# Four layer norms of a graph network: the last step moved to ScalarE, with the engines' sequences laid anew

## What is computed

```python
x = _layernorm(x + _L0_gnn_ref(x, adj, ...))   # attention, 4 heads of 64, masked by adj
x = _layernorm(x + _L1_gnn_ref(x, adj, ...))   # 4 heads: tanh of masked scores, times Wh, relu, then a gate
x = _layernorm(x + _L2_gnn_ref(x, adj, ...))   # 8 heads of 32: softmax cut where the cosine is at most 0.1
x = _layernorm(x + _L3_gnn_ref(x, adj, ...))   # attention, 4 heads of 64, masked by adj

def _layernorm(x, axis=-1, eps=1e-05):
    m = jnp.mean(x, axis=axis, keepdims=True)
    v = jnp.var(x, axis=axis, keepdims=True)
    return (x - m) / jnp.sqrt(v + eps)
```

## Time and profile before

| | us |
|---|---|
| median of 3 runs | 2612.17 |
| lowest, highest | 2611.11, 2615.91 |
| the profiled execution | 2615.28 |
| its span in the trace | 2613.5 |
| busy PE, DVE, ACT, POOL in it | 2549.5, 2006.1, 1394.8, 915.9 |

### The profile page before, as it was taken

One profiled execution on the slowest core, in us unless ns is written; L12 is line 12 of the kernel. 1 busy time (PEld: TensorE's weight loads), 2 busy tenths in 40 slices (PEclk: granted clock), 3 DMA queues, 4 the chain that ended last, 5 costly groups with the idle time before them and its releaser, 6 DMA issues.

```text
span 2613.5 us, 62943 instructions
## 1 busy us (share of the span) xinstructions
PE 2549.5 (98%) x21905; PEld 2283.8 (87%) x21905; DVE 2006.1 (77%) x6661; ACT 1394.8 (53%) x3893; POOL 915.9 (35%) x987
## 2 busy tenths in 40 slices
...
DMA packets 44490, 29.90 MB, mean 11 GB/s; under 512 B 21264, under 2 KB 44048, under 8 KB 44432
## 3 DMA queue, kind: packets, MB, share of 16 engines
...
## 4 chain that ended last, share of the span: by engine, by line
PE 83%; ACT 4%; DVE 3%; issue 1%; POOL 0%; DVEq 0%; ACTq 0%; POOLq 0%
PE bank L471 21%; PE bank L473 19%; PE bank L472 19%; ACT arena L603 4%; PE bank L1439 4%; PE bank L528 4%; PE bank L537 3%; PE bank L460 3%; PE bank L1429 3%; PE bank L548 2%; PE bank L1419 2%; PE bank L1450 2%; DVE arena L687 1%; DVE b L644 0%; DVE arena L644 0%
## 5 line engine op out<-in xcount | busy, mean ns | idle before, releaser
L402 POOL TENSOR_SCALAR l_ve<-l_mv 128x2 f32<-128x2 f32 x128 | 28.7, 225 | 1031.6 <-DVE l_mv L387 1031.4
L471 PE MATMUL bank<-arena_r 128*128 128x256 f32 x1024 | 303.7, 297 | 1.7 <-DVE g_c L1663 1.5
L1590 ACT ACTIVATE b<-b,s_sh 128x256 f32<-128x256 f32 x496 | 246.8, 503 | 89.1 <-DVE s_sh L644 89.1
L473 PE MATMUL bank<-arena_r 128*128 128x256 f32 x1024 | 289.5, 283 | 0.0
L472 PE MATMUL bank<-arena_r 128*128 128x256 f32 x1024 | 289.3, 282 | 0.0
L1868 POOL TENSOR_TENSOR arena_r<-a,arena_r 128x512 fp32r<-128x512 f32 x128 | 166.0, 1297 | 334.6 <-ACT arena_r L1531 334.6
L1863 POOL TENSOR_TENSOR arena_r<-a,arena_r 128x512 fp32r<-128x512 f32 x128 | 166.2, 1298 | 161.0 <-ACT arena_r L1537 160.7
L471 PEld LDWEIGHTS bank<-arena_r 128*128 128x128 f32 x1024 | 194.8, 190 | 24.1 <-issue 21.8
L1759 DVE SCALAR_TENSOR_TENSOR b<-bank,b 128x256 f32<-128x256 f32 x496 | 184.8, 420 | 32.0 <-ACT b L1590 25.9
L472 PEld LDWEIGHTS bank<-arena_r 128*128 128x128 f32 x1024 | 195.8, 191 | 0.0
L473 PEld LDWEIGHTS bank<-arena_r 128*128 128x128 f32 x1024 | 195.4, 191 | 0.0
...
## 6 DMA issues: line engine op xcount, KB each, us to landing
...
```

Source lines behind the costliest of these rows:

```text
L471: pe.matmul(out, w[0], x[0], start=first, stop=False)
L473: return pe.matmul(out, w[1], x[0], start=False, stop=last)
L1590: last = act.activation(R.e[h // QUAD][:, n, it, :], R.e[h // QUAD][:, n, it, :], ACT.Exp, bias=S.sh[:, it, h:h + 1], scale=-1.0, accum_ou ...
```

## The change

`dve_norm_out` is gone. In its place `act_norm_out` makes rs * x + nm on ScalarE, one Identity activation per tile, with scale and bias per node (`rs` and `nm`). For this POOL makes nm = -mean * rs, in two further small instructions: mn = -mean ahead of the epsilon, nm behind the power. The semaphore `eps` becomes `root`, raised twice per graph; `rstd`, for which the last step waits, is now raised by nm. The four norm_out stages leave DVE's lists and enter ACT's. All lists are laid anew; on PE the same 77 stages stand in the loop body, on POOL the same 22, DVE has 79 in place of 83 and ACT 66 in place of 62. The loop body starts at another point of the cycle, so FILL and DRAIN have other lengths.

```diff
-    N.eps = Signal(ctx, nc, f"{name}_eps")
+    N.root = Signal(ctx, nc, f"{name}_root", 2)
...
+    N.mn = ctx.enter_context(nc.sbuf_tensor(f"{name}_mn", [P, T], F32))
+    N.nm = ctx.enter_context(nc.sbuf_tensor(f"{name}_nm", [P, T], F32))
...
-def dve_norm_out(dve, N, g):
-    dve.wait_ge(N.rstd.sem, N.rstd.at(g))
+def act_norm_out(act, N, g):
+    act.wait_ge(N.rstd.sem, N.rstd.at(g))
     for it in range(T):
-        last = dve.tensor_scalar(N.r[:, it, :], N.r[:, it, :], N.mv[:, it, 0:1], N.rs[:, it:it + 1],
-                                 ALU.subtract, ALU.mult)
+        last = act.activation(N.r[:, it, :], N.r[:, it, :], ACT.Identity, bias=N.nm[:, it:it + 1], scale=N.rs[:, it:it + 1])
     last.then_inc(N.out.sem, 1)
...
 def pool_norm(pool, N, C, g):
     pool.wait_ge(N.var.sem, N.var.at(g))
     apart(pool)
-    pool.tensor_scalar(N.ve[:, :], N.mv[:, :, 1], LN_EPS, None, ALU.add).then_inc(N.eps.sem, 1)
-    pool.wait_ge(N.eps.sem, N.eps.at(g))
-    pool.tensor_tensor(N.rs[:, :], N.ve[:, :], C.minus_half[:, 0:T], ALU.pow).then_inc(N.rstd.sem, 1)
+    pool.tensor_scalar(N.mn[:, :], N.mv[:, :, 0], -1.0, None, ALU.mult)
+    pool.tensor_scalar(N.ve[:, :], N.mv[:, :, 1], LN_EPS, None, ALU.add).then_inc(N.root.sem, 1)
+    pool.wait_ge(N.root.sem, N.root.at(g, 1))
+    pool.tensor_tensor(N.rs[:, :], N.ve[:, :], C.minus_half[:, 0:T], ALU.pow).then_inc(N.root.sem, 1)
+    pool.wait_ge(N.root.sem, N.root.at(g, 2))
+    pool.tensor_tensor(N.nm[:, :], N.mn[:, :], N.rs[:, :], ALU.mult).then_inc(N.rstd.sem, 1)
```

Of ORDER's lists, two lines of ACT's before and of ACT's after:

```diff
-        ("b_copy_4", 3), ("g_p_3", 2), ("b_relu_1", 3), ("g_ha", 2), ("g_ha_t", 2), ("d_x_t", 3), ("a_x_t", 1),
+        ("g_p_3", 2), ("b_relu_1", 3), ("g_ha", 2), ("b_norm_out", 3), ("g_ha_t", 2), ("d_x_t", 3), ("g_gate", 2),
+        ("a_x_t", 1), ("d_k", 3), ("d_q", 3), ("g_norm_out", 2), ("d_exps_0", 3), ("d_exps_1", 3), ("d_exps_2", 3),
```

More of the change, by code:

```diff
@@ L52 @@
     "PE": [
[L53 to L57, removed]
@@ L58 @@
-        ("a_probs_3", 0), ("a_values_0", 0), ("a_values_1", 0), ("d_out", 2), ("a_out", 0), ("b_m", 1), ("b_k", 1),
-        ("b_q", 1), ("g_x_t", 0), ("g_adj_t", 0), ("b_sem", 1), ("g_wh_0", 0), ("g_z_0", 0), ("g_wh_1", 0),
[5 rows of a table removed]
[5 rows of a table added]
+        ("g_ha_1_1", 1), ("g_ha_3_0", 1), ("g_ha_3_1", 1), ("g_hf", 1), ("g_ha_t", 1), ("g_gate_x", 1), ("d_x_t", 2),
+        ("g_gate", 1), ("a_x_t", 0), ("d_k", 2), ("d_q", 2), ("d_v", 2), ("d_scores_0", 2), ("d_scores_1", 2),
[3 rows of a table added]
+        ("a_out", 0), ("g_adj_t", 0), ("b_m", 1), ("b_k", 1), ("b_q", 1), ("g_x_t", 0), ("b_sem", 1), ("g_wh_0", 0),
@@ L87 @@
[L87 to L90, removed]
+        ("b_factors", 3), ("b_scale", 3), ("b_sum", 3), ("b_stats", 3), ("g_diff", 2), ("g_ha_t", 2), ("d_x_t", 3),
@@ L110 @@
-        ("a_probs_1", 1), ("a_probs_2", 1), ("a_probs_3", 1), ("a_values_0", 1), ("a_values_1", 1), ("b_q", 0),
-        ("a_out", 1), ("b_sem", 0), ("g_adj_t", 1), ("b_unit_t", 0), ("b_scores_0", 0), ("g_x_t", 1), ("g_wh_0", 1),
[6 rows of a table removed]
-        ("d_x_t", 0), ("g_ha_3_1", 1), ("g_ha_3_0", 1), ("d_k", 0), ("g_ha_t", 1), ("a_x_t", 2), ("d_q", 0),
-        ("g_gate_x", 1), ("d_scores_0", 0), ("g_gate", 1), ("d_v", 0), ("a_q", 2), ("a_k", 2), ("d_scores_1", 0),
[3 rows of a table removed]
-        ("b_sem", 1), ("b_m", 1), ("g_x_t", 2), ("b_q", 1), ("b_k", 1), ("g_adj_t", 2), ("g_z_0", 2), ("g_wh_0", 2),
[6 rows of a table removed]
@@ L130 @@
-        ("g_ha_2_0", 2), ("g_ha_3_0", 2), ("g_hf", 2), ("g_ha_t", 2), ("g_gate_x", 2), ("d_x_t", 1), ("g_gate", 2),
-        ("a_x_t", 3), ("d_k", 1), ("d_q", 1), ("d_v", 1), ("d_scores_0", 1), ("d_scores_1", 1), ("a_v", 3),
[3 rows of a table removed]
-        ("a_out", 3), ("b_m", 2), ("b_k", 2), ("b_sem", 2), ("g_x_t", 3), ("g_adj_t", 3), ("b_q", 2), ("g_wh_0", 3),
[6 rows of a table removed]
+        ("w_qk", 0), ("a_probs_0", 0), ("a_probs_1", 0), ("w_col_r", 0), ("a_probs_2", 0), ("a_probs_3", 0),
+        ("a_values_0", 0), ("a_values_1", 0), ("w_col_qk", 0), ("a_out", 0), ("w_sem", 0), ("w_col_w", 0),
[4 rows of a table added]
@@ new lines @@
+        ("d_probs_3", 0), ("a_probs_2", 2), ("b_x_t", 1), ("a_probs_3", 2), ("a_values_0", 2), ("a_values_1", 2),
+        ("d_values_1", 0), ("g_adj_t", 2), ("a_out", 2), ("d_out", 0), ("b_q", 1), ("b_m", 1), ("b_sem", 1),
[7 rows of a table added]
+        ("g_gate_x", 2), ("d_x_t", 1), ("g_gate", 2), ("a_x_t", 3), ("d_q", 1), ("d_k", 1), ("d_v", 1),
[3 rows of a table added]
+        ("a_values_0", 3), ("a_values_1", 3), ("d_out", 1), ("a_out", 3), ("b_m", 2), ("b_k", 2), ("b_sem", 2),
+        ("g_x_t", 3), ("b_q", 2), ("g_wh_0", 3), ("g_z_0", 3), ("g_wh_1", 3), ("g_adj_t", 3), ("b_unit_t", 2),
@@ L142 @@
+        ("g_z_1", 3), ("b_scores_0", 2), ("g_s_0", 3), ("g_z_2", 3),
     ],
     "ACT": [
-        ("a_x_t", 0), ("w_map", 0), ("a_k", 0), ("a_q", 0), ("a_exps_0", 0), ("a_exps_1", 0), ("a_exps_2", 0),
[4 rows of a table removed]
-        ("g_p_3", 0), ("g_ha", 0), ("g_ha_t", 0), ("a_x_t", 1), ("g_gate", 0), ("a_k", 1), ("a_q", 1), ("b_x_t", 0),
-        ("a_exps_0", 1), ("a_exps_1", 1), ("a_exps_2", 1), ("a_exps_3", 1), ("a_probs_0", 1), ("a_probs_2", 1),
-        ("b_k", 0), ("a_o_copy", 1), ("b_q", 0), ("b_unit_t", 0), ("g_x_t", 1), ("b_exps_0", 0), ("b_exps_1", 0),
[5 rows of a table removed]
@@ new lines @@
+        ("g_p_2", 0), ("g_p_3", 0), ("g_ha", 0), ("g_ha_t", 0), ("a_x_t", 1), ("g_gate", 0), ("a_q", 1), ("a_k", 1),
+        ("g_norm_out", 0), ("b_x_t", 0), ("a_exps_0", 1), ("a_exps_1", 1), ("a_exps_2", 1), ("a_exps_3", 1),
+        ("b_q", 0), ("a_probs_0", 1), ("a_probs_2", 1), ("b_k", 0), ("a_o_copy", 1), ("a_norm_out", 1),
[5 rows of a table added]
+        ("g_p_3", 1), ("b_norm_out", 0), ("d_x_t", 0), ("g_ha", 1), ("d_k", 0), ("d_q", 0), ("g_ha_t", 1),
+        ("a_x_t", 2), ("d_exps_0", 0), ("g_gate", 1), ("d_exps_1", 0), ("a_q", 2), ("a_k", 2), ("d_probs_0", 0),
@@ L184 @@
-        ("g_norm_out", 1), ("a_o_copy", 2), ("d_o_copy", 0), ("b_x_t", 1), ("a_sum", 2), ("a_stats", 2), ("d_sum", 0),
-        ("a_norm_out", 2), ("b_m", 1), ("b_square", 1), ("g_x_t", 2), ("b_sem", 1), ("d_stats", 0), ("b_unit", 1),
-        ("g_z_0", 2), ("g_wh_0", 2), ("g_adj_t", 2), ("g_z_1", 2), ("b_mask_0", 1), ("b_mask_1", 1), ("b_mask_2", 1),
-        ("b_mask_3", 1), ("g_wh_1", 2), ("g_a_0", 2), ("d_norm_out", 0), ("b_cut_0", 1), ("g_z_2", 2), ("b_cut_1", 1),
+        ("a_x_t", 0), ("w_map", 0), ("a_v", 0), ("a_mask_0", 0), ("a_mask_1", 0), ("a_mask_2", 0), ("a_norm_p_0", 0),
```

170 lines of the change are left out of this document (88 added, 82 removed), and 249 rows, old and new, of tables (DRAIN, FILL, ORDER).

## The result

The changed kernel takes 2821.1 us (median of 4 runs, 2818.9 to 2821.7), the kernel before 2613.8 beside it; the ratio is 1.079, 95% interval 1.078 to 1.080. I had forecast 2639, with 2656 as the top of the range. The sign was right and the size wrong: 207 us in place of 27. The profiled execution has a span of 2819.9.

The account below looks back on a forecast made before the run. PE was taken to bound the kernel. Norm chains coming uncovered add 0.60 + 0.25 + 0.05 = 0.90 us over 28 turns (25.2), plus 2.3 at the end: +27.5, about 2639 us, range 2606 to 2656 (own range 2624 to 2656).

Parts of the forecast that it names:

- The bound and the sign: PE, busy 98% of the span, bounds the kernel; longer norm chains come out from under its queue; slower, chance 0.72.
- The fill and the drain are laid anew, with the same work; I count 0: Parts before and behind the loop: no change in time, give or take 3 us.
- my rivals: No change (2614 us, chance 0.15), faster (2599, 0.12), slower than forecast (2653, 0.13).
- my own sign: Test set beforehand: mechanism wrong if the turn stays as long as before or PE's new wait stands elsewhere.
- early enough: Layer "b"'s norm, needed by d_x_t on PE, ready at 1045.07, was to cause no wait there.
- What is free: DVE's eight fewer instructions (3.3 us per graph) hidden, b_x_t's 0.2 covered, no table load added.
- Place A: Norm of layer "a" to g_wh_0: 0.78 chain growth less 0.18 spare, +0.60 us per turn (0.3 to 0.8).
- The growth: Norm chain longer by mn 0.20, nm 0.30 and ACT's pair 0.28 over DVE's: 0.78 us (0.2 to 1.2).
- "slower" rival: POOL's small ops in layer "a"'s norm chain stretched by 0.5 a turn: 14 us more, 2653; chance 0.13.
- Place B: Norm of layer "b", between g_ha and g_ha_t: ACT's pair delays g_ha_t and g_gate, +0.25 us per turn (0.03 to 0.45).
- Place C: Norm of layer "g" ahead of d_exps on ACT: exponentials up to 0.5 late, counted +0.05 us per turn (0 to 0.3).
- The a_probs_2 wait: PE's wait at layer "a"'s last attention transposes, 0.48 us over normal distance, stays, as its chain is unchanged.

Follow-up runs that it names:

- e1: The changed kernel with eight already met semaphore waits added on DVE once, between FILL and the loop: 2677.6 us, ratio 1.024.
- e7: The changed kernel with eight added DVE waits, without POOL's negation of the mean (mn); nm made from the mean itself: 2634.9 us, ratio 1.009.
- e9: The kernel before with its old lists, norms' last step on ACT, and in the loop ACT does g_ha_t ahead of b_norm_out: 2693.9 us, ratio 1.031.
- e4: The changed kernel's lists, but the norms' last step on DVE and POOL's two instructions; d_norm_out behind g_z_0: 2741.2 us, ratio 1.049.
- e8: The changed kernel's lists, but the norms' last step on DVE and POOL's two instructions; d_norm_out behind b_mask_1: 2689.7 us, ratio 1.030.

## Why the prediction was right or wrong

**The bound and the sign: right.** PE bounds the kernel, and what counts is chains that come out from under its queue.

**The step that failed: "The fill and the drain are laid anew, with the same work; I count 0".** The list before the loop is 61 instructions longer on DVE in the compiled code, and that moved the loop's start from number 63 of a block to 124, where its 286 instructions touch four blocks. e1 against the changed kernel puts this at 143 us of the 206 of span: 137 in 25 turns, the rest in the head and the tail. None of my rivals had it. By my own sign, a new wait of PE elsewhere, the mechanism is wrong here: the largest new wait, 3.49 us, stands at d_x_t, which I had called early enough. "What is free" priced what stands on the engines, not where their code lies. Whether a new order falls into it is luck: of 128 places for the start, 29 make this body touch four blocks.

**The sum was too small besides.** Without the fetches the change takes 2677.6 us, still above the 2656 of my range. The parts follow.

**Place A: mechanism right, term too small.** 0.60 was forecast, PE lost 1.20 (0.98 at g_x_t, 0.22 at g_wh_0, by e1's starts against the kernel before). The spare time of 0.18 held: 1.43 of growth less 0.18 is 1.25. The growth was mis-sized in each part: mn 0.30 start to start in place of 0.20, nm 0.77 in place of 0.30, the pair 1.09 on ACT in place of 1.02 (+0.35 over DVE's 0.74 in place of +0.28). For mn the upper bound in my text was the true value; nm's collision was my "slower" rival in kind (a small POOL op stretched by 0.5 in this chain), on another instruction. I gave it 0.13 as a rival, where it was the case. Moving g_adj_t forward did only what I said, cover the norm and uncover the copies.

**Place B: mechanism right, term too small.** 0.25 forecast (0.03 to 0.45). In e1 g_gate's first matmul starts 0.60 us behind the one before it, where it was 0.14 in the kernel before: 0.46. e7 took 0.3 of it off when the chain there was 0.30 shorter, so mn's and the pair's errors count here too. e9 shows that it is ACT's queue that does it.

**Place C: right only while others hide it.** 0.05 forecast; e1's turn shows nothing there, e9's shows 0.6 as soon as B is mended.

**g_z_1, not in the sum.** PE's distance there is 0.60 us in e1 in place of 0.27, 0.33 more, and e7 gained 0.22 of it: DVE's low part of z, for which PE waits there, comes late with the norm. Places A, B and this one make 1.99; the turn grew by 1.85, so PE's other distances are 0.14 shorter in the new lists.

**The a_probs_2 wait: right.** It stays at 0.6 us between starts, in all kernels but e4 and e8, where it is 0.5.

**The turn without the fetches** is 79.90, 1.85 over 78.05 where I had 0.90, so 46 us in 25 turns. Head and tail are 6.7 and 10.6 us longer in e1 than before, where I had 2.3 in all. In part these are the same longer norms with nothing over them (the last d_x_t waits 5.5 in place of 4.6); how much the new lists add there was not tried.
